# A gated delta-rule layer on one core: V leaves PSUM in one copy, GpSimd scales it, and all queues are reordered

## The chip, the cores and the metric

The kernel runs on 1 core of one Trainium2 chip. The metric is the time on the device in microseconds. One core has TensorE (PE; its weight loads are shown as PEld), VectorE (DVE), ScalarE (ACT), GpSimd (POOL) and SyncE (SP), which here issues the DMAs. Each engine has its own queue and works through it in order; semaphores make one wait for another.

## The reference, cut to what matters

```python
q = _causal_conv_silu(x @ Wq.T, conv_q)   # 4 taps, then silu; 16 heads of 64
k = _causal_conv_silu(x @ Wk.T, conv_k)
v = _causal_conv_silu(x @ Wv.T, conv_v)   # 16 heads of 128
q, k = _l2_norm(q), _l2_norm(k)
alpha = exp(-exp(A_log) * softplus(x @ Wa.T + dt_bias)); beta = 2 * sigmoid(x @ Wb.T)
def step(S, inp):                          # one token, state S of 64 x 128 a head
    kS = einsum('bhd,bhdv->bhv', k_t, S)
    S = a_t * (S - b_t * einsum('bhd,bhv->bhdv', k_t, kS)) + einsum('bhd,bhv->bhdv', k_t, v_t)
    return S, einsum('bhdv,bhd->bhv', S, q_t)
...
return _rms_norm(o) @ Wo.T
```

Around it stand layer norms and residuals, and behind it a small feed-forward layer. x is 8 x 1024 x 128 in float32.

## The kernel before

The recurrence is done in chunks of 64 tokens. There are 8 pairs of heads and 16 chunks, so 128 steps; a step does one chunk of one head pair for all 8 batch rows. Within a chunk the recurrence is a triangular system: a gram matrix of the keys is masked, its diagonal 16x16 blocks are inverted, and four rounds of small matmuls complete the inverse.

Work of three steps is under way at once. Each engine has a body function that takes l, m, n (oldest, middle, newest step) and calls helpers in a fixed order written out by hand; a hardware loop repeats the body. What stands in that order is what the engine does next, whatever else is ready. The helpers that matter here, with their lines in the profile:

- `pe_proj` (L511): projections 0 to 3 are K, Q and two halves of V, all into PSUM banks 0 and 1. ScalarE's `act_tap0` (L720) takes the first tap out of PSUM, VectorE's `dve_conv` (L853) adds three more, and only then may the next projection start. SiLU and the square of K are L737 and L743.
- `pe_vtr` (L571) transposes V into PSUM. `act_v` (L766) takes it out into `Vt` in eight activations of 128 columns, each scaled by one column of `rv`, the reciprocal norm of the keys. VectorE's `dve_r` (L953) reads `Vt`.
- `pe_nk` (L521) sums the squares of K; `dve_n2`, `dve_r2` (L860, L868) and GpSimd's `pool_bn` and `pool_dmn` (L978, L999) make the factor with which `dve_n` (L891) turns the gram matrix (`pe_gram_k`, L544) into `Nd`. ScalarE's exp (L728) is the factor's other input.
- `Nd` goes to memory (`sp_gram`, L1102) and comes back as 16x16 blocks (`sp_gram_in`, L1110). GpSimd eliminates 8x8 blocks (`pool_elim`, L1053 to L1059); the four instructions of `dve_sub` (L922 to L932) on VectorE join them. `sp_z_out` and `sp_x_out` (L1116, L1122) write the results out, `sp_z_in` (L1130) and `sp_x_in` (L1137, L1138) read them in another layout.
- `pe_y` (L585), `pe_z` (L611), `pe_x` (L595) do the rounds of the inverse; z0 is the first `pe_z`. `pe_u` (L637) makes U, evicted by `act_u` (L797); `pe_o` (L650, L653) makes the output, `pe_ds` (L687) the state update, which `dve_s` (L961) adds to the decayed state `Sg` of GpSimd (L1013).
- GpSimd also makes `QG` (L1035) and a difference of decays, `pool_d` (L969), the first call of its body. SyncE loads G's factor for `QG` in `sp_g`.
- `pe_wo` (L707) applies the output weights to the oldest step, `act_yr` (L818) evicts the result.

The dictionary `PB` names the PSUM bank pair of each product. Bare waits in `pe_body` stand ahead of a call where the pair's last content has still to be read. In the kernel before, TensorE's order within a body is: projection 0, V transposes, gram_p, ks, projection 1, ms, norm of K, y0, gram_k, wo, z0, projection 2, y1, x, norm of Q, z1, projection 3, U, K transposes, O, state update.

Of the kernel before, what the change touches and what calls it, by code (L numbers as in the profile page):

```python
# [18 lines left out]
P = 128  # L19
NB = 8  # L20
# [60 lines left out]
def build(nc, x, wtab, wo, wab, hcol, cst, wf, mu, out):  # L81
    with ExitStack() as ctx:
# [312 lines left out]
        v_tr = sig("v_tr")  # L395
        v_ok = sig("v_ok")
# [59 lines left out]
        PB = {"nk": 2, "gk": 4, "nq": 4, "gp": 2, "ktr": 2, "vtr": 4, "y0": 6, "z0": 4, "x": 4, "y1": 6, "z1": 6, "ks": 6, "u": 6, "o": 4, "ds": 6, "ms": 4, "wo": 2}  # L456
# [536 lines left out]

        def pool_dmn(pool, n):
# [156 lines left out]
        def sp_body(sp, l, m, n):  # L1151
            if n is not None:
                sp_d(sp, n)
            if l is not None:
                sp_wo(sp, l)
            if m is not None:
                sp_g(sp, m)
            if n is not None:
                sp_wkq(sp, n)
            if m is not None:  # L1160
                sp_z_out(sp, m)
                sp_x_out(sp, m)
# [5 lines left out]
            if n is not None:  # L1168
                sp_gram(sp, n)
                sp_gram_in(sp, n)  # L1170

        def pe_body(pe, l, m, n):
            if n is not None:
                if m is not None:
                    pe.wait_ge(conv[3].sem, conv[3].at(m))
                pe_proj(pe, n, 0)
            if m is not None:
                if l is not None:
# [3 lines left out]
                pe_vtr(pe, m)  # L1182
                pe.wait_ge(kt_ok.sem, kt_ok.at(m))
                pe_gram_p(pe, m)
                pe_ks(pe, m)
# [3 lines left out]
            if l is not None:  # L1189
                if m is not None:  # L1190
                    pe.wait_ge(v_ok.sem, v_ok.at(m))
                else:
                    pe.wait_ge(oc_ok.sem, oc_ok.at(l))
                pe_ms(pe, l)
            if n is not None:
                if m is not None:
                    pe.wait_ge(pt_ok.sem, pt_ok.at(m))
                pe_nk(pe, n)
            if m is not None:
# [3 lines left out]
            if n is not None:  # L1203
                if l is not None:
                    pe.wait_ge(ro_in.sem, ro_in.at(l))
                elif m is not None:
                    pe.wait_ge(v_ok.sem, v_ok.at(m))
                pe_gram_k(pe, n)
            if l is not None:
                if n is not None:  # L1210
                    pe.wait_ge(n2_ok.sem, n2_ok.at(n))
                elif m is not None:
                    pe.wait_ge(pt_ok.sem, pt_ok.at(m))
                elif l is not None and not first(l):
                    pe.wait_ge(yr_ok.sem, yr_ok.at(l - 1))
                else:
                    pe.wait_ge(pt_ok.sem, pt_ok.at(l))
                pe_wo(pe, l)
            if m is not None:
                if n is not None:  # L1220
                    pe.wait_ge(nd_ok.sem, nd_ok.at(n))
                elif l is not None:
                    pe.wait_ge(ro_in.sem, ro_in.at(l))
                else:
                    pe.wait_ge(v_ok.sem, v_ok.at(m))
# [4 lines left out]
            if m is not None:  # L1230
                pe.wait_ge(y_ok.sem, y_ok.at(m, 1))
                pe_y(pe, m, 1)
                pe_x(pe, m)
                pe.wait_ge(x_ok.sem, x_ok.at(m))
                pe_nq(pe, m)
# [4 lines left out]
            if m is not None:  # L1240
                pe_u(pe, m, 0)
                pe_u(pe, m, 1)
            if n is not None:
                if l is not None:
                    pe.wait_ge(yr_ok.sem, yr_ok.at(l))
                else:
                    pe.wait_ge(n2_ok.sem, n2_ok.at(n))
                pe_ktr(pe, n)
# [410 lines left out]
```

## Time and profile before

| | us |
|---|---|
| median of 3 runs | 3398.29 |
| the runs | 3397.6 to 3399.78 |
| the profiled execution | 3398.14 |
| its span on the core | 3396.3 |

| engine | busy us | share of the span |
|---|---|---|
| PE | 2822.9 | 83% |
| ACT | 2654.5 | 78% |
| DVE | 2551.4 | 75% |
| POOL | 2053.6 | 60% |

The 128 steps take up most of the span: the first instruction of L969 starts at 102.2 us, the last at 3133.0. Ahead of them lies the layer norm and the decay tables, behind them the feed-forward layer. The steps look alike, so one of them, laid out engine by engine, stands for all. A timeline merges consecutive instructions of one line into one row; its start is that of the first, its duration reaches to the end of the last.

### The profile page before, as it was taken

Reading aid. Unit: us, or ns where it says so; the run is one execution under the profiler, and the core shown is the slowest. Engines: PE = TensorE matmul, PEld = TensorE weight load, DVE = VectorE, ACT = ScalarE, POOL = GpSimd, SP = SyncE. Lnnn points to the kernel's source line nnn. Section 1 sums busy time; section 2 is a strip of 40 time slices with the busy share of each in tenths; the row PEclk is TensorE's granted clock in tenths of the full one; section 3 lists DMA queues with packets and bytes.
Section 4 is the critical chain, followed back from the end, with each engine's and each line's share of the span. In section 5 each row is a group of like instructions: output and inputs, shape, how many; then the busy total and the mean of one; then the engine's idle time right before and its main releaser. Section 6 shows DMA issues by size and latency. Waiting matters only on the chain. (4 is left out here: it accounts for less than half of the span.)

```text
span 3396.3 us, 200052 instructions
## 1 busy us (share of the span) xinstructions
PE 2822.9 (83%) x80034; PEld 2335.4 (69%) x80034; DVE 2551.4 (75%) x5466; ACT 2654.5 (78%) x5678; POOL 2053.6 (60%) x3430
## 2 busy tenths in 40 slices
PE   6588888888888888888888888888888888888565
PEld 5477777777777777777777777777777777777443
DVE  6577778777777878787777878777787877777353
ACT  2588888888888888888888888888888888888453
POOL 1366666666666666666666666666666666666245
PEclk9699999999999999999999999999999999999787
DMA  2233333333333333333333333333333333333211
GB/s 65 67 80 79 79 84 80 82 77 81 80 78 81 81 83 78 81 77 80 80 79 83 80 83 77 81 80 78 81 82 83 78 81 80 79 80 80 47 44 38
DMA packets 931827, 260.24 MB, mean 77 GB/s; under 512 B 824256, under 2 KB 898240, under 8 KB 931776
## 3 DMA queue, kind: packets, MB, share of 16 engines
q1 hardware_dynamic: 931616, 259.01, 34.1%
q8 instruction: 34, 0.56, 0.1%
q0 software_dynamic: 160, 0.53, 0.0%
q14 instruction: 17, 0.14, 0.0%
HBM read 203.29 MB, written 56.11 MB: 76 GB/s over the span
## 5 line engine op out<-in xcount | busy, mean ns | idle before, releaser
L853 DVE SCALAR_TENSOR_TENSOR cv<-ps,w_v,cv 128x512 f32<-128x512 f32 x768 | 576.7, 751 | 401.7 <-ACT cv L720 383.6
L853 DVE SCALAR_TENSOR_TENSOR cv<-ps,w_kq,cv 128x512 f32<-128x512 f32 x768 | 575.4, 749 | 96.3 <-ACT cv L720 73.0
L511 PE MATMUL ps<-xnT,w_kq 128*128 (+1 forms) x1024 | 300.0, 414 | 111.9 <-DVE cv L853 94.6
L511 PE MATMUL ps<-xnT,w_v 128*128 (+1 forms) x1024 | 297.1, 411 | 82.0 <-DVE cv L853 69.3
L978 POOL TENSOR_TENSOR sc<-tabP,sc 128x8 f32<-128x8 f32 x128 | 26.1, 204 | 491.4 <-DVE sc L868 491.4
L511 PEld LDWEIGHTS ps<-xnT,w_kq 128*128 128x128 f32 x1024 | 173.9, 190 | 190.6 <-issue 169.7
L1013 POOL TENSOR_TENSOR Sg<-S,tabR 128x512 f32<-128x512 f32 x256 | 262.0, 1044 | 65.9 <-DVE S L961 65.9
L1022 POOL TENSOR_TENSOR accT<-accT,X 128x512 f32 (+1 forms) x128 | 163.7, 1279 | 220.1 <-ACT Y L818 220.1
L818 ACT ACTIVATE X<-ps,sc 128x128 f32<-128x128 f32 x512 | 145.9, 368 | 180.8 <-PE ps L707 180.8
L953 DVE SCALAR_TENSOR_TENSOR Rr<-ps,sc,Vt 128x128 f32<-128x128 f32 x1024 | 275.3, 342 | 0.8 <-ACT Vt L766 0.8
L766 ACT ACTIVATE Vt<-ps,sc 128x128 f32<-128x128 f32 x1024 | 272.2, 365 | 0.7 <-PE ps L571 0.7
L637 PEld LDWEIGHTS ps<-Rr,Z 64*64 64x64 f32 x4096 | 225.8, 134 | 66.5 <-issue 66.5
L637 PE MATMUL ps<-Rr,Z 64*64 64x128 f32 x4096 | 253.2, 273 | 16.1 <-ACT Z L789 1.9
L511 PEld LDWEIGHTS ps<-xnT,w_v 128*128 128x128 f32 x1024 | 173.9, 190 | 131.1 <-issue 109.8
L707 PE MATMUL ps<-wo_s,oo 128*128 128x128 f32 x2048 | 262.7, 282 | 0.0
L650 PE MATMUL ps<-QG,S 64*64 64x64 f32 x8192 | 208.4, 221 | 54.2 <-ACT U L797 54.2
L707 PEld LDWEIGHTS ps<-wo_s,oo 128*128 128x128 f32 x2048 | 238.3, 192 | 8.6
L653 PE MATMUL ps<-PT,U 64*64 64x64 f32 x8192 | 221.4, 221 | 25.0 <-PE ps L650 22.0
L650 PEld LDWEIGHTS ps<-QG,S 64*64 64x64 f32 x8192 | 194.6, 135 | 68.3 <-issue 68.3
L797 ACT ACTIVATE U<-ps 128x512 f32<-128x512 f32 x256 | 152.8, 597 | 104.2 <-PE ps L637 104.2
L1035 POOL TENSOR_TENSOR QG<-sl,ex 128x512 f32<-128x512 f32 x128 | 165.3, 1291 | 107.2 <-PE ps L653 107.2
L653 PEld LDWEIGHTS ps<-PT,U 64*64 64x64 f32 x8192 | 196.5, 135 | 39.2 <-issue 39.1
(201 smaller groups left out, 7928.7 us busy)
## 6 DMA issues: line engine op xcount, KB each, us to landing
Lm<-scrD SPq DMA_DIRECT2D x256, 128.0 KB, 3.0
scrN<-Nd SPq DMA_DIRECT2D x256, 128.0 KB, 2.6
ex<-scrG SPq DMA_DIRECT2D x256, 128.0 KB, 2.9
Z<-scrZ SPq DMA_DIRECT2D x256, 128.0 KB, 3.3
X<-scrX SPq DMA_DIRECT2D x512, 64.0 KB
w_kq<-wtab SPq DMA_DIRECT2D x128, 132.0 KB, 2.5
w_v<-wtab SPq DMA_DIRECT2D x128, 132.0 KB, 2.8
wo_s<-wo SPq DMA_DIRECT2D x128, 128.0 KB, 2.6
```

The costliest lines, as they stand in the source:

```text
L511: last = nc.tensor.matmul(pj[:, 4 * g:4 * g + 4, 0:CW], w[:, (j % 2) * P:(j % 2 + 1) * P], xnT3[:, 4 * g:4 * g + 4, bass.ds((n % NC) * C, ...
L637: last = nc.tensor.matmul(ps[a:z, col128(PB["u"], g, i)], blk64(BD["Z"], b, a), unit(Rr, b)[a:z], start=True, stop=True)
L650: last = nc.tensor.matmul(o_cols(h, b, d), S[a:z, b * P + d:b * P + d + 64], blk64(BD["QG"], b, a), start=(b == 0), stop=False)
L653: last = nc.tensor.matmul(o_cols(h ^ cls, b, d), U[a:z, b * P + d:b * P + d + 64], blk64(BD["PT"], b, a), start=False, stop=(b == NB - 1))
L707: last = nc.tensor.matmul(ps[:, col128(PB["wo"], h, i)], oo[:, h * 512 + i * P:h * 512 + (i + 1) * P], wo_s[:, h * D:(h + 1) * D], start=T ...
L766: last = nc.scalar.activation(unit(Vt, b), unit(ps, 4 * PB["vtr"] + b), ACT.Copy, scale=rv[:, b:b + 1])
L797: nc.scalar.activation(half(U, g), bank(PB["u"] + g), ACT.Copy).then_inc(u_oks[g].sem, 1)
L853: nc.vector.scalar_tensor_tensor(cv4[:, j], pj[:, :, k:k + C], tap(j, k), cv4[:, j], ALU.mult, ALU.add).then_inc(conv[j].sem, 1)
L953: last = nc.vector.scalar_tensor_tensor(unit(Rr, b), ps[:, col128(PB["ks"], g, i)], cr[:, b:b + 1], unit(Vt, b), ALU.mult, ALU.add)
L1013: nc.gpsimd.tensor_tensor(half(Sg, g).rearrange("p (b v) -> p b v", b=4), half(S, g).rearrange("p (b v) -> p b v", b=4), gam, ALU.mult).th ...
L1022: nc.gpsimd.tensor_tensor(dst, dst, row(yt[h]), ALU.add).then_inc(acc_ok.sem, 1)
L1035: nc.gpsimd.tensor_tensor(half(BD["QG"], 0), half(sl, 1), half(ex, 2), ALU.mult).then_inc(qg_ok.sem, 1)
```

## The change

`act_v` becomes one unscaled copy of 1024 columns out of two PSUM banks, which signals `v_cp`. A new function of GpSimd, `pool_v`, multiplies `Vt` in place by `rv`, broadcast over 128 columns, and signals `v_ok`. `act_v` no longer waits for `rv`. The PSUM bank pairs are dealt out anew, and the calls in all five bodies are put in a new order, with the bare waits that the new banks need.

TensorE's new order: projection 0, ms, ks, gram_p, projection 1, norm of K, wo, y0, gram_k, z0, projection 2, x, y1, K transposes, z1, projection 3, U (second half first), norm of Q, state update, O, V transposes of the newest step.

```diff
-        PB = {"nk": 2, "gk": 4, "nq": 4, "gp": 2, "ktr": 2, "vtr": 4, "y0": 6, "z0": 4, "x": 4, "y1": 6, "z1": 6, "ks": 6, "u": 6, "o": 4, "ds": 6, "ms": 4, "wo": 2}
+        PB = {"nk": 4, "gk": 4, "nq": 4, "gp": 4, "ktr": 6, "vtr": 6, "y0": 2, "z0": 2, "x": 6, "y1": 2, "z1": 2, "ks": 2, "u": 2, "o": 4, "ds": 2, "ms": 6, "wo": 6}
...
         def act_v(act, m):
             act.wait_ge(v_tr.sem, v_tr.at(m))
-            act.wait_ge(rv_ok.sem, rv_ok.at(m))
...
-            for b in range(NB):
-                last = nc.scalar.activation(unit(Vt, b), unit(ps, 4 * PB["vtr"] + b), ACT.Copy, scale=rv[:, b:b + 1])
-            last.then_inc(v_ok.sem, 1)
+            nc.scalar.activation(Vt[:], bank(PB["vtr"], 2), ACT.Copy).then_inc(v_cp.sem, 1)
...
+        def pool_v(pool, m):
+            pool.wait_ge(v_cp.sem, v_cp.at(m))
+            pool.wait_ge(rv_ok.sem, rv_ok.at(m))
+            Vt3 = Vt[:].rearrange("p (b d) -> p b d", b=NB)
+            nc.gpsimd.tensor_tensor(Vt3, Vt3, bcast(rv, P), ALU.mult).then_inc(v_ok.sem, 1)
...
         def sp_body(sp, l, m, n):
             if n is not None:
-                sp_d(sp, n)
+                sp_wkq(sp, n)
             if l is not None:
                 sp_wo(sp, l)
             if m is not None:
-                sp_g(sp, m)
-            if n is not None:
-                sp_wkq(sp, n)
+                sp_gram_in(sp, m)
+            if n is not None:
+                sp_d(sp, n)
             if m is not None:
                 sp_z_out(sp, m)
+            if n is not None:
+                sp_g(sp, n)
+            if m is not None:
                 sp_x_out(sp, m)
                 sp_z_in(sp, m)
...
                 sp_gram(sp, n)
-                sp_gram_in(sp, n)
...
         def pool_body(pool, l, m, n):
             if n is not None:
                 pool_d(pool, n)
             if m is not None:
+                pool_sq_q(pool, m)
                 pool_qg(pool, m)
+                pool_v(pool, m)
                 pool_sg(pool, m)
                 pool_nm(pool, m)
             if n is not None:
                 pool_bn(pool, n)
                 pool_dmn(pool, n)
-            if m is not None:
-                pool_sq_q(pool, m)
-            if n is not None:
-                pool_dmp(pool, n)
                 pool_cr(pool, n)
             if l is not None:
                 pool_acc(pool, l, 0)
             if n is not None:
+                pool_dmp(pool, n)
                 pool_xi(pool, n)
...
```

The bodies of ScalarE and VectorE after the change, in the loop:

```python
def act_body(act, l, m, n):
    act_tap0(act, n, 0); act_xb(act, m); act_oc(act, l); act_abs(act, n)
    act_silu_k(act, n); act_sq_k(act, n); act_tap0(act, n, 1)
    act.preload_act_table_set("natural_log_exp_and_others")
    act_exp(act, n); act_ro_ln(act, l); act_ro_exp(act, l); act_y(act, m, 0)
    act_yr(act, l); act_rv_ln(act, n); act_tap0(act, n, 2)
    act_x(act, m); act_y(act, m, 1); act_z1(act, m); act_tap0(act, n, 3)
    act_rv_exp(act, n); act_u(act, m, 1); act_u(act, m, 0)
    act.preload_act_table_set("silu_and_others")
    act_silu_q(act, n); act_silu_v(act, n, 0); act_silu_v(act, n, 1)
    act_osq(act, m); act_v(act, n)

def dve_body(dve, l, m, n):
    dve_conv(dve, n, 0); dve_p(dve, m); dve_ro_in(dve, l); dve_r(dve, m, 0)
    dve_n2(dve, n); dve_r2(dve, n); dve_r(dve, m, 1)
    dve_conv(dve, n, 1, 1, 3); dve_n(dve, n); dve_conv(dve, n, 1, 3, 4)
    dve_z0(dve, m); dve_conv(dve, n, 2); dve_conv(dve, n, 3); dve_nqs(dve, m)
    dve_k(dve, n); dve_sub(dve, n, 0, 2); dve_sub(dve, n, 2, 4)
    dve_s(dve, m, 0); dve_s(dve, m, 1)
```

Before, `dve_k` (L904, K's scaling) stood first in VectorE's body, `act_silu_v` first in ScalarE's, exp ahead of the Q tap, and `dve_sub` directly behind the last V taps.

## Rows read from the trace of the kernel before

**Rows 1.** The page: busy time, share and instructions of each engine.

```profile
PE 2822.9 (83%) x80034; PEld 2335.4 (69%) x80034; DVE 2551.4 (75%) x5466; ACT 2654.5 (78%) x5678; POOL 2053.6 (60%) x3430
```

**Rows 2.** Line 969: duration in ns (min/median/max), first and last start.

```profile
L969 POOL TENSOR_TENSOR Lm<-Lm,tabP x128: 1031/1123/1492, 102.2 to 3133.0; 128x512 f32<-128x512 f32 x128
```

**Rows 3.** Timeline, TensorE, one step: start us, us, operation [idle before <-releaser].

```profile
1484.91 1.15 PE L511 MATMUL ps<-xnT,w_v 128*128 x4
1486.19 1.85 PE L637 MATMUL ps<-Rr,Z 64*64 64x128 f32 x30
...
1489.04 0.34 PE L650 MATMUL ps<-QG,S 64*64 64x64 f32 x8 [0.42 <-ACT U L797]
...
1491.32 1.08 PE L687 MATMUL ps<-U,KT 64*64 64x128 f32 x32
1492.51 1.17 PE L511 MATMUL ps<-xnT,w_kq 128*128 x4
1493.66 1.09 PE L571 MATMUL ps<-k_all,sv 128*128 128x128 f32 x8
...
1500.36 0.69 PE L585 MATMUL ps<-Z,NM 64*64 64x64 f32 x32 [0.51 <-DMA Z<-scrZ]
1500.84 0.68 PE L544 MATMUL ps<-sl 64*64 64x64 f32 x32
1501.45 2.05 PE L707 MATMUL ps<-wo_s,oo 128*128 128x128 f32 x16
...
1504.37 1.15 PE L511 MATMUL ps<-xnT,w_v 128*128 x4 [0.24 <-DVE cv L853]
...
1508.89 1.15 PE L511 MATMUL ps<-xnT,w_v 128*128 x4 [0.23 <-DVE cv L853]
```

**Rows 4.** Timeline of the same step, ScalarE.

```profile
1486.10 0.69 ACT L720 ACTIVATE cv<-ps,w_v 128x512 f32<-128x512 f32 x1
...
1488.19 0.60 ACT L797 ACTIVATE U<-ps 128x512 f32<-128x512 f32 x1 [0.28 <-PE ps L637]
...
1497.59 0.63 ACT L743 ACTIVATE sq<-sl 128x512 f32<-128x512 f32 x1
```

**Rows 5.** Timeline of the same step, VectorE.

```profile
1489.22 0.68 DVE L922 TENSOR_TENSOR tmpS<-NS,XT 64x512 f32<-64x512 f32 x1
...
1491.74 0.68 DVE L932 TENSOR_REDUCE XT<-tmpS 64x64 f32<-64x512 f32 x1
...
1494.53 2.32 DVE L853 SCALAR_TENSOR_TENSOR cv<-ps,w_kq,cv 128x512 f32<-128x512 f32 x3
...
1502.09 0.69 DVE L891 TENSOR_TENSOR Nd<-ps,ex 128x512 f32<-128x512 f32 x1 [0.56 <-POOL ex L999]
1502.69 1.53 DVE L853 SCALAR_TENSOR_TENSOR cv<-ps,w_kq,cv 128x512 f32<-128x512 f32 x2
```

**Rows 6.** Groups by form: busy us, mean ns | idle before, releaser.

```profile
L766 ACT ACTIVATE Vt<-ps,sc 128x128 f32<-128x128 f32 x1024 | 272.2, 365 | 0.7 <-PE ps L571 0.7
...
L1035 POOL TENSOR_TENSOR QG<-sl,ex 128x512 f32<-128x512 f32 x128 | 165.3, 1291 | 107.2 <-PE ps L653 107.2
...
L809 ACT ACTIVATE oo<-ps 128x1024 f32<-128x1024 f32 x128 | 130.3, 1018 | 0.0
```

**Rows 7.** Timeline, all engines, 150.9 to 151.2.

```profile
150.98 1.04 POOL L969 TENSOR_TENSOR Lm<-Lm,tabP 128x512 f32<-128x512 f32 x1
...
151.13 1.44 DVE L922 TENSOR_TENSOR tmpS<-NS,XT 64x512 f32<-64x512 f32 x1 [0.34 <-POOL XT L1059]
```

**Rows 8.** Timeline, GpSimd, 1512 to 1516.

```profile
1513.62 1.13 POOL L969 TENSOR_TENSOR Lm<-Lm,tabP 128x512 f32<-128x512 f32 x1 [0.49 <-issue]
```

**Rows 9.** Timeline of the step of rows 3, SyncE's issues.

```profile
1495.96 1.27 SPq L1130 DMA_DIRECT2D Z<-scrZ  x2
...
1499.97 0.62 SPq L1138 DMA_DIRECT2D X<-scrX  x1
```

**Rows 10.** Line 1110, the gram load: landing of its DMAs.

```profile
DMA to landing us min/median/max: 2.5/2.6/4.1
```

More of the change, by code:

```diff
@@ L395, in build @@
         v_tr = sig("v_tr")
+        v_cp = sig("v_cp")
         v_ok = sig("v_ok")
@@ L1176, in pe_body @@
                 pe_proj(pe, n, 0)
+            if l is not None:
+                if m is not None:
+                    pe.wait_ge(v_cp.sem, v_cp.at(m))
+                else:
+                    pe.wait_ge(x_ok.sem, x_ok.at(l))
+                pe_ms(pe, l)
             if m is not None:
+                pe_ks(pe, m)
                 if l is not None:
@@ L1198, in pe_body @@
                 pe_nk(pe, n)
+            if l is not None:
+                pe.wait_ge(ro_in.sem, ro_in.at(l))
+                pe_wo(pe, l)
             if m is not None:
@@ L1203, in pe_body @@
             if n is not None:
[L1204 to L1207, printed above, removed]
+                pe.wait_ge(n2_ok.sem, n2_ok.at(n))
                 pe_gram_k(pe, n)
-            if l is not None:
-                if n is not None:
[L1211 to L1218, printed above, removed]
-            if m is not None:
[L1220 to L1225, printed above, removed]
+            if m is not None:
                 pe_z(pe, m, 0)
@@ L1230, in pe_body @@
             if m is not None:
-                pe.wait_ge(y_ok.sem, y_ok.at(m, 1))
-                pe_y(pe, m, 1)
-                pe_x(pe, m)
-                pe.wait_ge(x_ok.sem, x_ok.at(m))
-                pe_nq(pe, m)
+                if l is not None:
+                    pe.wait_ge(yr_ok.sem, yr_ok.at(l))
+                else:
+                    pe.wait_ge(v_cp.sem, v_cp.at(m))
+                pe_x(pe, m)
+                pe_y(pe, m, 1)
+            if n is not None:
+                if m is not None:
+                    pe.wait_ge(x_ok.sem, x_ok.at(m))
+                pe_ktr(pe, n)
+            if m is not None:
                 pe_z(pe, m, 1)
@@ L1266, in act_body @@
                 act_xb(act, m)
-                act_v(act, m)
+            if l is not None:
+                act_oc(act, l)
             if n is not None:
+                act_abs(act, n)
                 act_silu_k(act, n)
                 act_sq_k(act, n)
+                act_tap0(act, n, 1)
             act.preload_act_table_set("natural_log_exp_and_others")
@@ L1273, in act_body @@
                 act_exp(act, n)
[L1274 removed]
             if l is not None:
                 act_ro_ln(act, l)
+                act_ro_exp(act, l)
             if m is not None:
                 act_y(act, m, 0)
+            if l is not None:
+                act_yr(act, l)
             if n is not None:
                 act_rv_ln(act, n)
[L1281 to L1285 removed]
                 act_tap0(act, n, 2)
             if m is not None:
+                act_x(act, m)
                 act_y(act, m, 1)
[L1289 removed]
+                act_z1(act, m)
+            if n is not None:
+                act_tap0(act, n, 3)
+                act_rv_exp(act, n)
+            if m is not None:
+                act_u(act, m, 1)
+                act_u(act, m, 0)
             act.preload_act_table_set("silu_and_others")
@@ L1307, in dve_body @@
                 dve_p(dve, m)
-                dve_r(dve, m, 0)
-                dve_r(dve, m, 1)
             if l is not None:
                 dve_ro_in(dve, l)
+            if m is not None:
+                dve_r(dve, m, 0)
             if n is not None:
@@ L1314, in dve_body @@
                 dve_r2(dve, n)
-                dve_conv(dve, n, 1, 1, 2)
+            if m is not None:
+                dve_r(dve, m, 1)
+            if n is not None:
+                dve_conv(dve, n, 1, 1, 3)
                 dve_n(dve, n)
-                dve_conv(dve, n, 1, 2, 4)
+                dve_conv(dve, n, 1, 3, 4)
             if m is not None:
```

56 lines of the change are left out of this document (15 added, 41 removed).

## The prediction

> **What bounds the kernel now.** I read the page's line of busy times first. No engine is full: TensorE, the busiest, works 83% of the span and ScalarE 78% [rows 1]. So relieving ScalarE is worth nothing by itself; the question is which closed ring of waits sets the length of a step. The 128 starts of one instruction that runs once a step lie 23.87 us apart on average (102.2 to 3133.0, 127 gaps) [rows 2]. Then I laid one step (1484.91 to 1508.89) out engine by engine [rows 3 to 5]. The ring runs through the four projections, which share two PSUM banks: projection, first tap on ScalarE, three taps on VectorE, next projection. Where nothing else interferes such a link takes 4.34 us from the projection to the end of its taps (1492.51 to 1494.53+2.32=1496.85) [rows 3, 5]. Two of the four links are stretched: from projection 3 to projection 0 7.60 us pass, with U, O and the state update between them on TensorE, and from the end of the K taps (1496.85) to projection 2 (1504.37) 7.52 us. The change reorders just what lies in these two stretches.
>
> **The operations that change.** V's copy: eight activations of 365 ns, 272.2 us in all, or 2.13 a step, become one of 1024 columns, of which the same shape takes 1018 ns [rows 6]. ScalarE is relieved of 1.1 us a step. GpSimd gets a 128x1024 multiply. The trace has none, so it is bounded: twice a 512-column form with a broadcast factor, 2 x 1.04 = 2.08 [rows 7], or twice the form with two full operands, 2 x 1.29 = 2.58 [rows 6]. Nearest is the first, since the factor here is broadcast too. On its own it lies beside other work: in my layout it starts some 9.5 to 10 us after projection 3, ends by 12.6 even at the dear end, and VectorE asks for V at 13.4 or later.
>
> **The ring in the new order.** I start at projection 3, at 0, and add only what depends on what came before.
> (1) To U: a group of matmuls frees the array 0.07 us before its modelled end if the next uses another number of rows (gram_k to wo: 0.61 for 0.68), so 1.15-0.07=1.08; now it is 1.28. (2) U and its two evictions, from 1486.19 to 1488.19+0.60: 2.60. (3) ScalarE to TensorE, as now before O: 1489.04-1488.79=0.25. (4) The state update now stands ahead of O. Between groups of 64-row tiles the next starts about one matmul early (y0 to gram_k: 0.48 for 0.69); for 128 columns that is 1.08-0.24=0.84. (5) O: 2.28 to a 64-row group, and 0.14 more to a 128-row one (0.61 against 0.48, rounded up): 2.42. (6) The V transposes, now ahead of projection 0: 1.09 plus the 0.11 that projection 0 now starts behind the end of its forerunner (1491.32+1.08 to 1492.51): 1.20; without this seam 1.02 [rows 3, 4]. That is 8.39 us where there are 7.60 now: the transposes have moved into this stretch.
> (7) Projection 0 to the end of the K taps: 4.34, now at 12.73. (8) silu and square: the square ends at 1498.22, 1.37 later [rows 4, 5]. (9) To the norm matmuls 0.15 (as tap end 1504.22 to projection 2 at 1504.37), norm to wo 0.61, wo to y0 2.05-0.07=1.98, y0 to gram_k 0.48, gram_k's end and hand-over 0.68+0.06. This reaches 18.06. Now wo comes behind gram_k and y0; in the new order wo stands ahead. (10) Nd 0.60, one tap 0.75, hand-over 0.15: projection 2 at 19.56, 6.83 behind the K taps where it was 7.52 [rows 3, 5]. Two other paths arrive at Nd at almost the same time, so shortening wo would not help: VectorE's own queue (the norm, half of R, two taps: about 17.9) and exp, which now stands behind the Q tap and a table load, then GpSimd's decay factor (about 18.0). (11) Projection 2 to 3: a link of 4.34 less 0.10 (ScalarE's first tap starts 1.19 behind projection 3, 1486.10, where it takes 1.29 behind projection 0) plus 0.15 for the hand-over, some 4.38; in the shown step 4.52, since the scaled evictions of yr were in the way [rows 3 to 5].
> Sum 8.39+4.34+6.83+4.38=23.94, 0.07 above the present step. The reordering by itself buys nothing: ScalarE's gain lies in idle time.
>
> **What it newly runs into.** Block inversion by VectorE: four dependent instructions from 1489.22 to 1491.74+0.68, 3.20 us [rows 5]. Now they wait for GpSimd's elimination. In the new order K's scaling precedes them, and it waits for the state update, that is until 3.93+1.08=5.01, so they start at 5.01+0.05+0.62=5.68, and with S behind them (1.20) VectorE is free at 10.1; the K taps want it at 10.41. The slack is 0.26. GpSimd starts the difference instruction (line 969) 10.84 us after the end of Nd (1502.78 to 1513.62) [rows 5, 8]; the two gram DMAs and the elimination between them keep their order. New: 18.06+0.69+10.84-23.94=5.65. So two instructions that both read two SBUF operands start within 0.03 us of each other. What then happens the trace shows most plainly near its start: GpSimd's instruction began at 150.98 (1.04 long), VectorE's L922 at 151.13 took 1.44 instead of 0.68: it lost 0.76 of the 0.89 that the other had left [rows 7]. So the second waits for the first, less some 0.14. GpSimd first costs VectorE 0.7; 0.26 is slack, 0.45 enters the ring. VectorE first costs GpSimd some 0.5 and the ring nothing directly. I take GpSimd first: any delay of projection 2 moves GpSimd's start forward against projection 3, and there is one, next. The price is between 0 and 0.65.
> The page "SBUF — State Buffer" of the Trainium skill, section "SBUF: two separate sides", says that VectorE with two SBUF inputs and GpSimd take an exclusive lock for the whole instruction. By that rule the loss would be the full remainder, 0.14 a step and 18 us in all on top of the forecast; the trace shows the lock but a smaller loss.
>
> **SyncE's queue.** The two G loads move from before the w_kq load to between Z's and X's outputs, and wait there for QG of the same step. The queued multiply and square are delayed by the collision, QG ends at about 10.0 and inversion at about 9.6, so, with SyncE's issues of about 0.6 and its gaps of 0.2 to 0.3, Z goes out at 9.7, G's issues end at 11.8, X goes out at 12.0 and Z is read from 12.85. The last X load is issued 4.01 us later (1495.96 to 1499.97) [rows 9], at 16.9, and lands 2.6 after that (X's own landing is not given, that of the gram load of equal size is) [rows 10], so z0 can begin at 19.6. Its turn by TensorE's order would be 18.8; behind it, 0.63 later, projection 2 at 20.2 instead of 20.0: about 0.1 more. Bounds: 0 (X lands 0.2 sooner) to 0.5 (G and Z loads slow each other).
>
> **Sum.** 0.07+0.45+0.1, 0.62 us for each of 126 steps: 78 us. Start and tail (some 370 us) keep their work. On the profiled span of 3396.3 us this gives 3474; that execution took 3398.14 us, 1.8 more than its span, and the median of the runs, 3398.29, is practically the same. Forecast 3476 us.
>
> **Rivals.**
> A, slower by the ring alone: VectorE gets in first, or the 0.26 slack is larger. Then 0.07 and, with G still ahead of X, 0 to 0.25: 3407 to 3439. For it: the two starts are 0.03 apart and the gram load's landings scatter by more (2.5 to 4.1) [rows 10]. Against: X's lateness pushes the collision to the bad side.
> B, faster: the seams on TensorE vanish. If the transposes reach projection 0 in 1.02 rather than 1.20 and U to state update takes 0.15 rather than 0.25 (as other hand-overs do), the ring is 23.66, 0.2 under the present one, and without a collision the time is 3370 to 3385. It decides at a ring under 23.85. For it: seams are read to 0.05 and there are eleven. Against: nearly every other unknown can only add.
> C, not what it says: GpSimd's multiply, queued ahead of Sg, the mask and the norm factors, becomes the bound. That needs it to take over 3.4 us, since V is asked for at 13.4; each us beyond costs 126 us. Against: both bounds lie below.
> D, worse: G, Z and X loads disturb one another so that y0 waits too; y0 has about 0.4 of slack behind Z's landing. With another 0.5 us a step: 3515 to 3550.
>
> **How the numbers follow.** Forecast case (3450 to 3500) 0.5, A 0.24, B 0.11, C 0.02, D 0.10, near no change 0.03. A measurement of this kernel can tell about 0.2% (7 us) from no change. Faster: B, 0.11. Same, 3391.5 to 3405: 0.03 and the lower edge of A, 0.09 in all. Slower: the rest, 0.80. Eight in ten: leave out B, and the upper part of D and C: 3396 to 3515.
>
> **What would show it.** Step length near 24.5; projection 3 to 0 near 8.4 and the V transposes directly ahead of projection 0; L922's mean well over 0.68 us with GpSimd's difference instruction just ahead; z0 released by the X loads; ScalarE busy 140 us less in sum, with its idle time up by more. Wrong: a step of 23.7 or less (my seams), L922 still at 0.68 (no collision), or V's consumer on VectorE waiting for GpSimd (C).

## The result and the profile after

| | before | after |
|---|---|---|
| median us, 4 runs each, taken in turn on one chip | 3399.03 | 3479.53 |
| the runs | 3397.6 to 3402.02 | 3474.58 to 3482.1 |
| span of the profiled execution | 3396.3 | 3477.0 |

The ratio is 1.0234, with a 95% interval of 1.0216 to 1.0252: 80.5 us slower. The forecast was 3476 us. The size came out almost as forecast; the terms of the sum did not, as the part on the prediction shows.

The page's line of busy times of the kernel after, which answers to [rows 1]:

```profile
PE 2819.4 (81%) x80034; PEld 2378.7 (68%) x80034; DVE 2597.8 (75%) x5466; ACT 2552.1 (73%) x4782; POOL 2419.6 (70%) x3558
```

ScalarE does 102 us less work and idles more. GpSimd does 366 us more: 242.6 are the new multiply, a longer QG adds 85 (165.3 in [rows 6], 250.7 now), a longer square 59, and some other rows are a little shorter. Nothing is full, so again the length of a step decides. The row of the line that was 969 and is 967 now (duration in ns, minimum, median, maximum; first and last start), to be held against [rows 2]:

```profile
L967 POOL TENSOR_TENSOR Lm<-Lm,tabP x128: 1032/1045/1545, 102.2 to 3214.5; 128x512 f32<-128x512 f32 x128
```

127 gaps in 3112.3 us are 24.51 us each, against 23.87: 0.64 a step, 81 us in all. What lies ahead of the first start and behind the last is as long as it was. So the whole loss is in the steps. In the rows below L512 is a projection, L638 U, L688 the state update, L572 the V transposes, L586 and L612 the matmuls y and z, L708 the output weights, L851 VectorE's taps, L902 K's scaling, and L920 to L930 the inversion. One step in the kernel after, TensorE's timeline (start us, us, operation, in brackets the idle time before it and who ended it), where [rows 3] has one of before:

```profile
1520.69 1.15 PE L512 MATMUL ps<-xnT,w_v 128*128 x4 [0.31 <-DVE cv L851]
...
1524.47 1.10 PE L688 MATMUL ps<-U,KT 64*64 64x128 f32 x32 [0.28 <-issue]
...
1527.78 1.09 PE L572 MATMUL ps<-k_all,sv 128*128 128x128 f32 x8
1528.70 1.08 PE L512 MATMUL ps<-xnT,w_kq 128*128 x4
...
1539.95 0.69 PE L612 MATMUL ps<-Y,X 64*64 64x64 f32 x32 [1.15 <-DMA X<-scrX]
1540.58 1.18 PE L512 MATMUL ps<-xnT,w_v 128*128 x4
...
1544.99 1.15 PE L512 MATMUL ps<-xnT,w_v 128*128 x4 [0.31 <-DVE cv L851]
```

From projection 3 (1520.69) to projection 0 it is 8.01 us, to projection 2 19.89, to the next projection 3 24.30. Projection 2 now starts directly behind z0, and z0 waited 1.15 us for the X loads. The waits of the whole trace (total us, times, longest):

```profile
PE ps L612 <- DMA X<-scrX: 172.8, 127, 3.1
```

On the mean that is 1.36 us a step. The shown step has 0.21 less than the mean, and is shorter than the mean step by just as much (24.30 and 24.51). VectorE and GpSimd in the same step, answering to [rows 5, 7, 8]:

```profile
1526.44 1.21 DVE L920 TENSOR_TENSOR tmpS<-NS,XT 64x512 f32<-64x512 f32 x1
...
1531.26 2.31 DVE L851 SCALAR_TENSOR_TENSOR cv<-ps,w_kq,cv 128x512 f32<-128x512 f32 x3
...
1539.58 0.74 DVE L851 SCALAR_TENSOR_TENSOR cv<-ps,w_kq,cv 128x512 f32<-128x512 f32 x1
```

```profile
1526.06 1.04 POOL L967 TENSOR_TENSOR Lm<-Lm,tabP 128x512 f32<-128x512 f32 x1 [0.50 <-issue]
1527.06 1.49 POOL L990 TENSOR_TENSOR sq<-sl 128x512 f32<-128x512 f32 x1
1528.52 2.01 POOL L1039 TENSOR_TENSOR QG<-sl,ex 128x512 f32<-128x512 f32 x1
1530.48 1.90 POOL L996 TENSOR_TENSOR Vt<-Vt,sc 128x1024 f32<-128x1024 f32 x1
```

GpSimd's difference instruction gets in first, and the inversion's first instruction (L922 before, L920 now) takes 1.21 us where it took 0.68 [rows 5]. I call this the collision. GpSimd pays too: its square runs beside the end of L920, and its QG, which starts 0.12 us behind L927 (1528.40), takes 2.01 us where it took 1.29 on the mean before [rows 6]. So the collisions also make QG late, for which the G loads wait. Over all 128 (the row of L920: minimum, median, maximum in ns, first and last start):

```profile
L920 DVE TENSOR_TENSOR tmpS<-NS,XT x128: 673/1199/1529, 124.3 to 3240.6; 64x512 f32<-64x512 f32 x128
```

SyncE's queue, answering to [rows 9], with the two G loads (L1092) ahead of X's output and everything behind it:

```profile
1531.07 1.18 SPq L1092 DMA_DIRECT2D ex<-scrG  x2
1532.37 0.63 SPq L1126 DMA_DIRECT2D scrX<-XB  x1
1533.21 1.32 SPq L1134 DMA_DIRECT2D Z<-scrZ  x2
...
1537.36 0.62 SPq L1142 DMA_DIRECT2D X<-scrX  x1
```

### The profile page after: what moved, and what is told of

Its sections match the earlier page's. It is cut to its first block and busy times, and to the rows that moved or that the text cites. A ratio compares the mean times of both kernels' runs of the same rounds, so it can differ in the third digit from the quotient of the medians.

```text
span 3477.0 us, 198784 instructions
## 1 busy us (share of the span) xinstructions
PE 2819.4 (81%) x80034; PEld 2378.7 (68%) x80034; DVE 2597.8 (75%) x5466; ACT 2552.1 (73%) x4782; POOL 2419.6 (70%) x3558
## 5 line engine op out<-in xcount | busy, mean ns | idle before, releaser
L851 DVE SCALAR_TENSOR_TENSOR cv<-ps,w_v,cv 128x512 f32<-128x512 f32 x768 | 576.8, 751 | 370.6 <-ACT cv L721 352.4
L851 DVE SCALAR_TENSOR_TENSOR cv<-ps,w_kq,cv 128x512 f32<-128x512 f32 x768 | 572.2, 745 | 28.1 <-ACT cv L721 14.5
L512 PE MATMUL ps<-xnT,w_kq 128*128 (+1 forms) x1024 | 287.6, 402 | 75.0 <-DVE cv L851 69.1
L512 PE MATMUL ps<-xnT,w_v 128*128 (+1 forms) x1024 | 304.6, 419 | 43.7 <-DVE cv L851 43.4
L721 ACT ACTIVATE cv<-ps,w_v 128x512 f32<-128x512 f32 x256 | 176.0, 687 | 198.5 <-PE ps L512 198.5
L612 PE MATMUL ps<-Y,X 64*64 64x64 f32 x8192 | 179.1, 223 | 175.0 <-DMA X<-scrX 172.8
L951 DVE SCALAR_TENSOR_TENSOR Rr<-ps,sc,Vt 128x128 f32<-128x128 f32 x1024 | 287.0, 343 | 0.0
L612 PEld LDWEIGHTS ps<-Y,X 64*64 64x64 f32 x8192 | 151.4, 135 | 189.6 <-issue 189.6
L708 PE MATMUL ps<-wo_s,oo 128*128 128x128 f32 x2048 | 264.3, 283 | 1.4 <-DVE sc L880 1.4
L638 PE MATMUL ps<-Rr,Z 64*64 64x128 f32 x4096 | 253.1, 273 | 1.0 <-ACT Z L787 1.0
L638 PEld LDWEIGHTS ps<-Rr,Z 64*64 64x64 f32 x4096 | 222.0, 133 | 46.2 <-issue 46.2
L1039 POOL TENSOR_TENSOR QG<-sl,ex 128x512 f32<-128x512 f32 x128 | 250.7, 1959 | 1.1 <-PE ps L654 1.0
L512 PEld LDWEIGHTS ps<-xnT,w_kq 128*128 128x128 f32 x1024 | 174.4, 190 | 110.6 <-issue 89.8
L708 PEld LDWEIGHTS ps<-wo_s,oo 128*128 128x128 f32 x2048 | 239.9, 193 | 10.2 <-issue 1.6
L996 POOL TENSOR_TENSOR Vt<-Vt,sc 128x1024 f32<-128x1024 f32 x128 | 242.6, 1895 | 2.5 <-ACT Vt L765 2.3
L512 PEld LDWEIGHTS ps<-xnT,w_v 128*128 128x128 f32 x1024 | 175.4, 191 | 87.7 <-issue 57.2
L1060 POOL TENSOR_TENSOR tmpE<-NS,XT 64x24 f32<-64x24 f32 (+3 forms) x768 | 188.2, 245 | 60.4
L1063 POOL TENSOR_TENSOR XT<-XT,tmpE 64x24 f32<-64x24 f32 (+3 forms) x768 | 179.4, 234 | 60.2
```

The source lines that it names most:

```text
L512: last = nc.tensor.matmul(pj[:, 4 * g:4 * g + 4, 0:CW], w[:, (j % 2) * P:(j % 2 + 1) * P], xnT3[:, 4 * g:4 * g + 4, bass.ds((n % NC) * C, ...
L612: last = nc.tensor.matmul(ps[a:z, col64(PB["z1" if l else "z0"], cls, i)], BD["X" if l else "X0"][q, b * C:(b + 1) * C], BD["Y"][q, b * C: ...
L638: last = nc.tensor.matmul(ps[a:z, col128(PB["u"], g, i)], blk64(BD["Z"], b, a), unit(Rr, b)[a:z], start=True, stop=True)
L708: last = nc.tensor.matmul(ps[:, col128(PB["wo"], h, i)], oo[:, h * 512 + i * P:h * 512 + (i + 1) * P], wo_s[:, h * D:(h + 1) * D], start=T ...
L851: nc.vector.scalar_tensor_tensor(cv4[:, j], pj[:, :, k:k + C], tap(j, k), cv4[:, j], ALU.mult, ALU.add).then_inc(conv[j].sem, 1)
L951: last = nc.vector.scalar_tensor_tensor(unit(Rr, b), ps[:, col128(PB["ks"], g, i)], cr[:, b:b + 1], unit(Vt, b), ALU.mult, ALU.add)
```

## The experiments

Two things may hold projection 2 back: SyncE's queue, which makes z0 wait for X, and the collision, which delays K's taps. Times of steps below are counted from projection 3 (L512) of the step shown. A step's mean length is worked out, as above, from the first and last start of GpSimd's difference instruction. "The changed kernel" is the one after, at 3479.53 us.

**G loads behind the X loads.** This takes away the first of the two alone, SyncE's queue.

```diff
             if m is not None:
                 sp_z_out(sp, m)
-            if n is not None:
-                sp_g(sp, n)
-            if m is not None:
                 sp_x_out(sp, m)
...
             if n is not None:
+                sp_g(sp, n)
                 sp_gram(sp, n)
```

> The changed kernel with SyncE's G loads moved from between Z's and X's outputs to behind the X loads. My theory: in the changed kernel z0 waits about 0.9 us for X and projection 2 starts 0.26 us a step late. Without G ahead of them Z and X are read 1.3 us sooner, z0 starts in its turn, and at least 0.26 us a step go: 33 us, to about 3447. If the earlier projection 2 also moves GpSimd's difference instruction behind the start of VectorE's inversion in part of the steps, more goes, down to 3410. Rival (the ring through the transposes alone is what got longer, SyncE's order is idle talk): 3470 to 3480, z0 still late or late without effect.

3418.8 us, 1.0057 [1.004, 1.0074]: 61 us of the 80 are gone. Step 24.01 on the mean. The collision stays, and this trace shows both of its outcomes in two steps that follow each other. GpSimd's rows of the two, then VectorE's:

```profile
1522.95 1.54 POOL L967 TENSOR_TENSOR Lm<-Lm,tabP 128x512 f32<-128x512 f32 x1 [0.50 <-ACT sl L752]
...
1546.53 1.04 POOL L967 TENSOR_TENSOR Lm<-Lm,tabP 128x512 f32<-128x512 f32 x1 [0.50 <-ACT sl L752]
```

```profile
1522.91 0.67 DVE L920 TENSOR_TENSOR tmpS<-NS,XT 64x512 f32<-64x512 f32 x1
...
1546.56 1.56 DVE L920 TENSOR_TENSOR tmpS<-NS,XT 64x512 f32<-64x512 f32 x1
```

At 1522.9 VectorE is 0.04 us ahead and keeps its 0.67, GpSimd takes 1.54; that step is 23.65 long (projection 3 at 1517.16 and 1540.81). One step later GpSimd is 0.03 ahead, and VectorE takes 1.56. So the order of two starts within 0.04 us decides who pays, and when GpSimd pays, the ring does not. Over all 128 steps (duration in ns, minimum, median, maximum) it is mostly GpSimd now, where in the changed kernel it was mostly VectorE:

```profile
L920 DVE TENSOR_TENSOR tmpS<-NS,XT x128: 672/675/1570, 123.5 to 3175.4; 64x512 f32<-64x512 f32 x128
L967 POOL TENSOR_TENSOR Lm<-Lm,tabP x128: 1031/1456/1597, 101.9 to 3150.8; 128x512 f32<-128x512 f32 x128
```

So the 61 us are not the queue's alone. L920's mean fell from 1139 to 984 ns; over 128 steps that is an estimated 20 us that came by way of the collision.

**K's scaling between the two halves of the inversion.** This goes at the collision: VectorE begins the inversion sooner, before GpSimd's instruction.

```diff
             if n is not None:
-                dve_k(dve, n)
                 dve_sub(dve, n, 0, 2)
+                dve_k(dve, n)
                 dve_sub(dve, n, 2, 4)
```

> The changed kernel with VectorE's scaling of K moved from ahead of the inversion to between its two halves, so the inversion starts as soon as GpSimd's elimination ends (0.8 us sooner) and its first instruction is not caught by GpSimd's difference instruction. My theory (collision of instructions with two SBUF operands costs 0.62 us a step): L920-like first instruction back to 0.68 us; the second multiply of the inversion then meets GpSimd's square and may lose 0.4, so the gain is 0.3 to 0.6 us a step: 3400 to 3441. Rival (the inversion is late because of K's scaling alone, no collision): the first instruction was 1.19 for another reason and stays so; gain about 0.6 from the earlier start at most. Rival (seams on TensorE): no gain, 3470 to 3480.

3443.42 us, 1.0131 [1.0114, 1.0147]; step 24.21. VectorE's timeline, one step:

```profile
1534.44 0.68 DVE L920 TENSOR_TENSOR tmpS<-NS,XT 64x512 f32<-64x512 f32 x1 [0.49 <-POOL XT L1063]
...
1536.37 1.51 DVE L927 TENSOR_TENSOR tmpS<-XT,tmpW 64x512 f32<-64x512 f32 x1
```

L920 is at 0.68 again, but the second multiply of the inversion, L927, meets GpSimd's next instruction and takes 1.51 (1.05 where it is alone, as the version with the wait and the late G shows below). The collision was moved, and less of it reaches the ring: K's taps start at 10.06 in this step (1539.71, projection 3 at 1529.65) and at 10.20 in the median one, where they started at 10.57. The queue is as it was, with waits of z0 as long as in the changed kernel:

```profile
PE ps L612 <- DMA X<-scrX: 169.2, 127, 2.9
```

Projection 2 starts 0.38 us behind the end of the taps in the median step; 0.15 is what it takes where nothing else holds it.

**Both of these edits.**

> Both edits of the two runs before. My theory: the gains add up, since one lies in the link from projection 2 on and the other in the one ahead of the K taps: 0.55 to 0.9 us a step, 3370 to 3410, so about the kernel before or a little faster. The ring that is left without both is 24.49-0.62-0.26=23.61 us a step as the changed kernel's trace shows it. Rival (only one of the two is on the ring at a time): the sum is no better than the better one of the two.

3442.06 us, 1.0118 [1.0101, 1.0135]: a miss by over 30 us, and no better than the second edit alone. TensorE's and VectorE's timelines of a step that starts at 1505.48:

```profile
1512.84 1.09 PE L572 MATMUL ps<-k_all,sv 128*128 128x128 f32 x8 [0.20 <-DVE KT L902]
1513.77 1.17 PE L512 MATMUL ps<-xnT,w_kq 128*128 x4
```

```profile
1512.04 0.67 DVE L902 TENSOR_TENSOR KT<-ps,tabP 128x512 f32<-128x512 f32 x1
1512.63 1.50 DVE L927 TENSOR_TENSOR tmpS<-XT,tmpW 64x512 f32<-64x512 f32 x1
```

K's scaling now waits for the first half of the inversion, that for GpSimd's elimination, and the V transposes for the PSUM banks that K's scaling reads. Projection 0 comes at 8.29 instead of 8.01. L927 still collides, at 1.50, and K's taps start at 10.48 (1515.96), where the second edit alone had them at 10.06. Without G in front of X, projection 2 is back at 0.15 behind the taps' end in the median step, so the queue no longer holds it; but the later taps cost as much as that gives.

**GpSimd's difference instruction without an SBUF operand.** This kernel leaves out the difference of decays: a memset of the same 128x512 tile stands in its place.

```diff
-            nc.gpsimd.tensor_tensor(v3(Lm, 1), v3(Lm, 0),
-                                    tabP3[:, bass.ds(n, 1), 0:8].rearrange("p o b -> p b o").to_broadcast([P, NB, C]),
-                                    ALU.subtract).then_inc(d_ok.sem, 1)
+            nc.gpsimd.memset(half(Lm, 1), 0.5).then_inc(d_ok.sem, 1)
```

> The changed kernel with GpSimd's difference of decays replaced by writing a constant: the difference is left out, so the decays are wrong, and all other work and waits stay. It reads no SBUF operand and is shorter. Theory of the collision: the inversion's first instruction takes 0.68 us instead of 1.19, K's taps start up to 0.6 sooner, minus what the next collision (second multiply against QG) gives back; 0.3 to 0.55 us a step, 3410 to 3440. If that instruction keeps 1.19 us, its length has nothing to do with GpSimd's operands and the theory falls.

3433.3 us, 1.0097 [1.008, 1.0114]; step 24.10. GpSimd's and VectorE's timelines:

```profile
1525.90 0.53 POOL L967 MEMSET Lm<- 128x512 f32 x1 [0.39 <-issue]
```

```profile
1526.11 0.67 DVE L920 TENSOR_TENSOR tmpS<-NS,XT 64x512 f32<-64x512 f32 x1
```

The two run side by side for 0.32 us and neither is longer for it. Over all 128 steps L920's median is 673 ns. So what makes VectorE wait is GpSimd's reading of SBUF (or its kind of instruction, which this run doesn't tell apart), not that GpSimd is at work. The memset also ends GpSimd's chain earlier, so the gain of 46 us isn't the collision's alone.

**GpSimd waits for K's scaling before the difference.** One wait makes the order of the two certain: VectorE is first.

```diff
             if n is not None:
+                if m is not None:
+                    pool.wait_ge(kt_ok.sem, kt_ok.at(m))
                 pool_d(pool, n)
```

> The changed kernel with one wait more: GpSimd's difference instruction waits for VectorE's scaling of K, which ends about when the inversion's first instruction starts, so VectorE always gets in first. Nothing is left out and nothing moved. Theory of the collision: the inversion's first instruction at 0.68 us in all steps, K's taps at 10.06 after projection 3 as in the run with the constant written; X still late by 0.3 to 0.4, since the G loads now wait for a later QG. 0.25 to 0.5 us a step less than the changed kernel: 3415 to 3445. If delaying an engine gains nothing, the collision was not on the ring (3475 to 3490).

3474.18 us, 1.0211 [1.0196, 1.0227]: only 5 us less than the changed kernel, which the intervals of the two ratios (1.0216 to 1.0252 for the changed kernel) hardly tell apart, and a clear miss. TensorE in one step:

```profile
1520.01 1.15 PE L512 MATMUL ps<-xnT,w_v 128*128 x4 [0.54 <-DVE cv L851]
...
1536.88 0.69 PE L586 MATMUL ps<-Z,NM 64*64 64x64 f32 x32 [0.35 <-DMA Z<-scrZ]
...
1539.25 0.69 PE L612 MATMUL ps<-Y,X 64*64 64x64 f32 x32 [1.21 <-DMA X<-scrX]
1539.87 1.18 PE L512 MATMUL ps<-xnT,w_v 128*128 x4
```

VectorE and GpSimd in that step:

```profile
1525.77 0.67 DVE L920 TENSOR_TENSOR tmpS<-NS,XT 64x512 f32<-64x512 f32 x1
...
1530.07 2.31 DVE L851 SCALAR_TENSOR_TENSOR cv<-ps,w_kq,cv 128x512 f32<-128x512 f32 x3
```

```profile
1529.06 1.28 POOL L1039 TENSOR_TENSOR QG<-sl,ex 128x512 f32<-128x512 f32 x1
```

The collision is gone and the K taps start at 10.06, 0.51 earlier than in the changed kernel (10.57). But projection 2 starts at 19.86, where it was 19.89. GpSimd's chain starts later and QG ends at 10.33 instead of 9.84; the G loads wait for it, X behind them, and z0 comes at 19.24. With QG made that late, the SyncE queue alone holds the step as long as both causes together do.

**The wait, and G behind X.**

> The wait of the run before and the G loads behind the X loads. In the run with late G loads alone most steps took 23.64 us and about one in ten 24.5, with the first instruction of the inversion at 0.68 in the short ones. My theory: the long ones are those in which GpSimd got in first; with the wait all steps are 23.64, which is 0.19 below the 23.83 of a step of the kernel before: 3368 to 3380, ratio 0.991 to 0.995. Rival (the long steps come from late DMA landings): the spread stays and the time is that of late G alone, 3410 to 3420.

3374.26 us (5 runs), 0.9925 [0.9911, 0.9938]: faster than both kernels, by 25 us than the one before and by 105 than the changed one. Its step, TensorE:

```profile
1522.04 1.15 PE L512 MATMUL ps<-xnT,w_v 128*128 x4 [0.50 <-DVE cv L851]
...
1530.06 1.08 PE L512 MATMUL ps<-xnT,w_kq 128*128 x4
...
1540.29 0.69 PE L612 MATMUL ps<-Y,X 64*64 64x64 f32 x32 [0.65 <-DMA X<-scrX]
1541.30 1.15 PE L512 MATMUL ps<-xnT,w_v 128*128 x4 [0.32 <-DVE cv L851]
...
1545.67 1.15 PE L512 MATMUL ps<-xnT,w_v 128*128 x4 [0.61 <-DVE cv L851]
```

VectorE:

```profile
1529.21 1.05 DVE L927 TENSOR_TENSOR tmpS<-XT,tmpW 64x512 f32<-64x512 f32 x1
...
1532.09 2.31 DVE L851 SCALAR_TENSOR_TENSOR cv<-ps,w_kq,cv 128x512 f32<-128x512 f32 x3
...
1540.41 0.74 DVE L851 SCALAR_TENSOR_TENSOR cv<-ps,w_kq,cv 128x512 f32<-128x512 f32 x1
```

GpSimd, one row of this step and L967 over all:

```profile
1529.33 1.78 POOL L990 TENSOR_TENSOR sq<-sl 128x512 f32<-128x512 f32 x1
```

```profile
L967 POOL TENSOR_TENSOR Lm<-Lm,tabP x128: 1032/1043/1292, 102.4 to 3112.7; 128x512 f32<-128x512 f32 x128
```

The shown step is 23.63 us long. Most are within 0.02 of that, and a few longer ones bring the mean to 23.70. GpSimd's square still meets L927 and pays for it, off the ring. Against the run before, only the place of the G loads differs: the last X load is issued at 15.64 instead of 16.59, and from there to z0 it is 2.61 and 2.65 us, so it is the queue's order and not slower transfers that made the 100 us. z0 is still released by X, with 0.65 us of idle ahead of it, but that wait costs nothing here: projection 2 waits for VectorE's taps, 0.15 behind their end. The same kind of row decides in the changed kernel and doesn't in this one; what tells them apart is the next row.

**V's copy alone, in the order of before.** Against the kernel before: one copy, the multiply put between GpSimd's decayed state and its mask product, all else as it was.

```diff
-            act.wait_ge(rv_ok.sem, rv_ok.at(m))
...
-            for b in range(NB):
-                last = nc.scalar.activation(unit(Vt, b), unit(ps, 4 * PB["vtr"] + b), ACT.Copy, scale=rv[:, b:b + 1])
-            last.then_inc(v_ok.sem, 1)
+            nc.scalar.activation(Vt[:], bank(PB["vtr"], 2), ACT.Copy).then_inc(v_cp.sem, 1)
...
+                pool_v(pool, m)
```

> The kernel before, in its old order and with its old banks, with the first part of the change alone: one unscaled copy of 1024 columns and GpSimd's multiply between the decayed state and the mask of the gram matrix. My theory: ScalarE's 1.1 us is idle time gained; V is ready at 13.0 after projection 3 where VectorE asks at 12.4, so R, the norm and what hangs on it come 0.2 to 0.4 us later a step: 3405 to 3445. Rival (ScalarE's load bounds the kernel): up to 1.1 us a step less, 3260 to 3390.

3422.4 us, 1.0067 [1.0051, 1.0082], 23 us slower than before. GpSimd and VectorE in a step that starts at 1497.84:

```profile
1508.86 1.90 POOL L996 TENSOR_TENSOR Vt<-Vt,sc 128x1024 f32<-128x1024 f32 x1 [0.42 <-ACT Vt L765]
```

```profile
1510.85 2.16 DVE L951 SCALAR_TENSOR_TENSOR Rr<-ps,sc,Vt 128x128 f32<-128x128 f32 x8 [0.55 <-issue]
```

The multiply ends at 1510.76 and R (L951), its consumer, starts 0.09 behind that. In the old order the copy comes late, and its round over GpSimd is on VectorE's path.

**The order alone, V scaled by ScalarE as before.** Against the changed kernel: eight scaled activations, no multiply.

```diff
+            act.wait_ge(rv_ok.sem, rv_ok.at(m))
...
-            nc.scalar.activation(Vt[:], bank(PB["vtr"], 2), ACT.Copy).then_inc(v_cp.sem, 1)
+            for b in range(NB):
+                last = nc.scalar.activation(unit(Vt, b), unit(ps, 4 * PB["vtr"] + b), ACT.Copy, scale=rv[:, b:b + 1])
+            last.then_inc(v_cp.sem, 1)
...
-                pool_v(pool, m)
```

> The changed kernel with its new order and banks, but V scaled by ScalarE in eight activations as before and without GpSimd's multiply: the second part of the change alone. In the new order V's eviction stands between O's square and the first K tap. With 2.1 instead of 1.02 us there, the tap starts at about 10.2 instead of 9.2 and K's taps on VectorE at 10.95 instead of 10.56: 0.3 to 0.5 us a step more than the changed kernel, 3510 to 3545. Rival (the two parts are independent): 3475 to 3485.

3505.45 us, 1.0309 [1.0293, 1.0325], 26 us over the changed kernel and a little less than expected. K's taps start at 11.00 (1516.32, projection 3 at 1505.32), 0.43 later than in the changed kernel: ScalarE's eviction of V, 2.17 us in this trace, stands ahead of K's first tap.

**The same edit on the fast version.** The wait and the late G, with V scaled by ScalarE.

> The fastest kernel so far (new order, G loads late, GpSimd's difference behind K's scaling) with V scaled by ScalarE in eight activations and no multiply on GpSimd. Theory: in the new order ScalarE's eviction of V lies on the ring once nothing else holds VectorE: V out by 10.3, first tap 10.3 to 11.0, K's taps from 11.0 instead of 10.06, so 0.9 us a step more than that kernel: 3480 to 3495. The single copy is then worth 110 us there, though it is worth nothing in the old order. Rival (copy worth the 40 us it showed in the changed kernel): 3410 to 3425.

3496.5 us, 1.0285 [1.0268, 1.0302]. ScalarE's and VectorE's timelines of a step that starts at 1503.78:

```profile
1512.00 2.18 ACT L767 ACTIVATE Vt<-ps,sc 128x128 f32<-128x128 f32 x8
```

```profile
1514.79 2.32 DVE L854 SCALAR_TENSOR_TENSOR cv<-ps,w_kq,cv 128x512 f32<-128x512 f32 x3 [0.88 <-ACT cv L721]
```

ScalarE's long eviction stands ahead of K's first tap and pushes the K taps to 11.01, from 10.05. The single copy is worth 122 us here, against 26 in the changed kernel and less than nothing in the old order.

**G moved in the kernel before.** Only SyncE's order of the kernel before is changed: its G loads go between Z's and X's outputs.

```diff
-            if m is not None:
-                sp_g(sp, m)
...
                 sp_z_out(sp, m)
+            if n is not None:
+                sp_g(sp, n)
+            if m is not None:
                 sp_x_out(sp, m)
```

> The kernel before with its G loads alone moved to where the change puts them, between Z's and X's outputs. In the old order QG ends at 8.07 after projection 3 and the block for X is ready at 10.07, so both G issues (8.6 to 9.8) fit into a gap of SyncE: no change, 3393 to 3406, X's last load still at 15.0. Rival (the place of the G loads costs by itself, through the memory traffic of X and Z): 10 us or more slower.

3401.47 us (10 runs), 1.0008 [0.9998, 1.0017]: no difference that these runs show. SyncE in a step that starts at 1509.46:

```profile
1517.86 1.17 SPq L1088 DMA_DIRECT2D ex<-scrG  x2
1519.55 0.64 SPq L1122 DMA_DIRECT2D scrX<-XB  x1
```

QG ends at 7.99 here, and the G loads are issued by 9.57, half a microsecond before X goes out at 10.09. So in the old order QG is made early enough that the same place in the queue is free; in the changed kernel it ends at 9.84. The place is bad only together with the new order; that QG standing behind the square on GpSimd is what does it was not tested by itself.

## Why the prediction was right, and where its terms were not

**What bounds the kernel** held. ScalarE lost 102 us of work and the kernel slowed down; the four projections are the ring. (I had forecast 140 us less. The eviction of V did fall by 141, from 272.2 [rows 6] to 131.1; why the engine's sum fell by less was not followed up.) A link without interference was put at 4.34; from 1528.03 to the end of the K taps at 1532.38 the kernel with the one wait shows 4.35.

**Step (1) to (6), projection 3 to projection 0: 8.39 forecast, 8.01 measured.** This is the largest error of the sum. U's eviction to the state update was given 0.25 as the hand-over ahead of O; from the start of projection 3 to the state update it is 3.78 (1524.47-1520.69), where my steps give 1.08+2.60+0.25=3.93; the hand-over itself is 0.09, from the end of U's eviction at 1524.38. State update and O held: 3.31 to the V transposes (1524.47 to 1527.78) for 0.84+2.42=3.26. But the V transposes to projection 0 take 0.92 (1527.78 to 1528.70), not 1.20: the 0.11 had been read behind the state update, another kind of group, and does not go with projection 0 to its new place. Both errors are what rival B named.

**Steps (7) to (11) held.** In the fast version the taps of K end at 1534.40 and projection 2 starts at 1541.30: 6.90 for a forecast of 6.83. From there to projection 3 it is 4.37 for 4.38.

**So "the reordering by itself buys nothing" was wrong.** The bare ring is 8.02+4.34+6.90+4.37=23.63 in the shown step and 23.70 on the mean, which is 0.17 below the old mean of 23.87, not 0.07 above it. It took the version with both disturbances removed to see this: 3374.26 us, inside rival B's 3370 to 3385. B's condition was that the seams vanish and no collision occurs; the seams did, the collision did not. Order and copy make this together: the order without the copy is at 3496.5 us, the copy without the order at 3422.4.

**The collision: 0.45 forecast, 0.52 measured, by other parts.** Forecast: 0.7 lost, less 0.26 of slack (10.41 less 10.1 is 0.31, so the term was also added up a little too high). In the shown step 0.53 is lost, since GpSimd starts 0.38 ahead and not beside VectorE (1526.06 and 1526.44), and there is no slack: in the fast version, without a collision, the K taps start at 10.05, just as VectorE comes free, and ScalarE's first tap is out only 0.15 sooner (1531.94). Projection 0 being 0.38 earlier had used the slack up. K taps in the changed kernel: 10.57. The rule "the rest of the other's time less some 0.14", taken from [rows 7], gave the loser's time well: 1.04-0.38=0.66 of rest and 0.53 lost here; in the two steps of the first experiment 0.63 and 0.50 (GpSimd loses, if its 1.04 is the time alone), 1.01 and 0.89. "GpSimd first" held for most steps: the median of L920 is 1199 ns, that of L967 1045. For GpSimd's square behind L927 the rule is a little off: in the fast version 0.93 of L927 was left at 1529.33 and the square took 1.78 for the 1.04 that it takes alone, so 0.74 was lost, 0.19 less than the rest.
The page "SBUF — State Buffer" of the Trainium skill, section "SBUF: two separate sides", says that the one that starts first holds the shared ports for its whole instruction and the other fully blocks, and that VectorE's two SBUF inputs count only against a GpSimd operation that reads SBUF. The second half agrees with the memset at 1525.90, beside which L920 kept its 0.67. The first half holds less exactly: the later one does wait, but pays 0.12 to 0.19 less than the whole of what the other had left.

**SyncE's queue: 0.1 forecast, more measured.** The last X load was to be issued at 16.9 and z0 to start at 19.6, 0.8 behind its turn at 18.8. Measured 16.67, 19.26 and a turn at 18.11 (z0's start less its 1.15 of waiting): the wait is longer, as the turn moved with the ring. Without X projection 2 could have started 0.15 behind the taps' end at 1540.32, at 19.78; it started at 19.89, so 0.11 of delay in the shown step, and the mean step waits 0.21 more. (My own numbers, 20.2 for 20.0, gave 0.2; the sum took 0.1.) Together with the 0.04 by which the last link is longer, the shown step is 0.52+0.11+0.04=0.67 over 23.63. The means of the changed and the fast version, 24.51 and 23.70, are 0.81 apart, where I had 0.55.

**The sum came out by compensation.** By the means, the ring was 0.24 too dear (23.94 for 23.70) and what it runs into 0.26 too cheap (0.55 for 0.81): 0.62 forecast over the old step, 0.64 measured. That the two errors cancel is luck; the direction and the two disturbances were forecast for the right reasons.

**Adding the two was the error of kind.** I added the collision and the queue as terms in a row. They are two chains that meet at projection 2, and the later sets it. From the changed kernel, taking away the collision alone gives about 5 us, the queue alone 61, both 105 us. From the fast version, putting in the queue alone costs 100 us, the collision alone (in the part of the steps in which GpSimd gets in first) 45, both 105. And whichever is taken away moves the other: a wait of GpSimd ends the collision but makes QG late; a sooner projection 2 alters the few hundredths by which one engine is ahead at L920. The "0.1" for X was the price behind a collision that already delayed everything, not its own price, which is 0.8 a step (100 us by 126) where the wait is in and QG is late.

**The other rivals.** C: the multiply takes 1.90 us, below my lower bound of 2.08, and ends at 11.69, ahead of its consumer's turn; it is hidden, as forecast. In the old order it isn't (0.55 us of idle time ahead of R). D: in the new order y0 waits for Z to any extent only in the kernel with the one wait (0.35 us in the shown step, 26 us in the whole trace), where it doesn't lead to more than 3474 us. A, VectorE first at 3407 to 3439: its condition was made certain by the one wait, with G still ahead of X, and the time was 3474.18 us. The 0 to 0.25 that A allowed for X was too little by the same error.

**Left open.** Why L967 ends up ahead of L920 in some steps of the first experiment and behind it in others was not traced to its origin; the landings of the gram loads between them scatter [rows 10]. How the 46 us of the memset are shared between the missing collision and GpSimd's shorter chain was not separated. An order in which QG stands ahead of the square on GpSimd was not tried, nor GpSimd's reading of SBUF with another kind of instruction.

## What to carry to other kernels

When a hand-written order is changed, price each newly late transfer by itself, with the other disturbances thought away, and then ask which chain reaches the meeting point last; don't add the delays. Read what a queue holds behind its first waiting entry: two loads that wait for QG held X's output and seven loads behind them, and putting them last gave 61 us, a part of it through the collision. Where two engines' instructions exclude each other and start within some hundredths of a microsecond, fix their order by a wait, so that the one with slack loses, and check what is queued behind the loser.

## What the runs showed of the hardware that was not expected

- A multiply of GpSimd in place, 128x1024 with a broadcast factor, takes 1.90 us; its 512-column forms with a broadcast factor take 1.04 [rows 7], so one long instruction is 0.18 cheaper than two.
- The exclusion between VectorE and GpSimd runs both ways and is short of whole by 0.12 to 0.19 us: 0.66 of rest cost VectorE 0.53, 1.01 cost it 0.89, 0.63 cost GpSimd 0.50, and 0.93 cost GpSimd's square 0.74. A GpSimd memset beside the same VectorE instruction costs neither anything (0.53 and 0.67 us, overlapping by 0.32).
- A projection that follows the V transposes starts 0.92 us after them, 0.17 ahead of their modelled end; behind the state update, in the old order, it started 0.11 behind the end [rows 3]. A seam on TensorE goes with what stands ahead, and is to be read for each new pair.
